# Layer norm ahead of linear attention and routed experts: 1/std by logarithm, exponential and a shorter Newton step, and the row normalisation split between VectorE and GpSimd

## What is computed

```python
xn = _layernorm(x)                       # (x - mean) / sqrt(var + 1e-5)
# attention: 16 heads of 8, feature map elu(a) + 1
q, k = elu(xn @ Wq.T) + 1, elu(xn @ Wk.T) + 1;  v = xn @ Wv.T
out = einsum(q, einsum(k, v)) / (q . sum(k) + 1e-6) @ Wo.T
# experts: 8 of them, one for each token
aff = xn @ centroids.T;  e = argmax(aff);  alpha = sigmoid(aff[e])
h = relu(_layernorm(xn, ln_g[e], ln_b[e]) @ w1[e].T + b1[e])
y = alpha * (xn + h @ w2[e].T + b2[e]) + (1 - alpha) * xn
```

## Time and profile before

| | us |
|---|---|
| median of 3 runs | 171.39 |
| lowest, highest | 169.41, 172.38 |
| time of the profiled execution | 170.78 |
| its span in the profile | 169.1 |
| busy: TensorE, VectorE, ScalarE, GpSimd | 139.1, 113.6, 104.9, 101.0 |

### The profile page before, as it was taken

How to read it: one execution, slowest core, us unless ns; L and a number is a source line. 1 busy time by engine, 2 the same in 40 slices (tenths; PEclk the granted TensorE clock), 3 DMA queues, 4 the chain that set the end, 5 groups by cost and what they waited for, 6 DMA issues and landing times.

```text
span 169.1 us, 4618 instructions
## 1 busy us (share of the span) xinstructions
PE 139.1 (82%) x1106; PEld 128.8 (76%) x1106; DVE 113.6 (67%) x411; ACT 104.9 (62%) x332; POOL 101.0 (60%) x108
## 2 busy tenths in 40 slices
PE   0066698999976987888799798999999999999950
PEld 0055597899944865766799688999999999999940
DVE  3899776999964865869756565666676665555540
ACT  8487996999252763556365647666676765566520
POOL 7600000899675655466235461888788868777884
PEclk9999999999999999999999999999999999999998
DMA  4999100680038765153234784698888878844433
GB/s 136 322 301 386 43 0 0 216 297 4 4 94 254 223 193 144 40 136 65 82 96 150 200 252 154 158 176 171 180 167 161 168 166 183 150 70 40 44 33 31
DMA packets 19113, 24.05 MB, mean 142 GB/s; under 512 B 2576, under 2 KB 13328, under 8 KB 18960
## 3 DMA queue, kind: packets, MB, share of 16 engines
q1 hardware_dynamic: 13456, 19.50, 36.2%
q0 software_dynamic: 5632, 4.26, 19.9%
HBM read 17.40 MB, written 6.36 MB: 140 GB/s over the span
## 4 chain that ended last, share of the span: by engine, by line
PE 53%; DVE 19%; issue 7%; ACT 7%; POOL 6%; another core or an unknown queue 2%; DMA 2%; DVEq 1%; ACTq 0%
PE bank L623 18%; PE bank L611 18%; POOL out L354 6%; PE bank L579 5%; PE bank L569 2%; ACT xn L401 2%; PE bank L596 2%; PE bank L515 2%; DVE feat_q L886 2%; PE bank L506 2%; PE bank L587 2%; DVE lane_neg L810 2%; PE bank L603 2%; DMA x<-in_x 2%
## 5 line engine op out<-in xcount | busy, mean ns | idle before, releaser
L470 ACT ACTIVATE hT<-bank,b 128x128 f32<-128x128 f32 x156 | 44.5, 368 | 29.6 <-PE bank L611 25.7
L354 POOL DMA_INDIRECT out<-rows,token_at x32 | 50.0, 1563 | 15.1 <-DVE rows L925 9.0
L346 POOL DMA_INDIRECT rows<-z_rows,token_at x32 | 30.6, 958 | 25.0 <-PE bank L611 11.5
L623 PE MATMUL bank<-w,hT 128*128 x312 | 42.8, 280 | 3.2 <-ACT hT L470 1.8
L623 PEld LDWEIGHTS bank<-w,hT 128*128 128x128 f32 x312 | 37.8, 191 | 5.2 <-issue 4.9
L611 PE MATMUL bank<-zT,feat_k 128*128 128x128 f32 x312 | 41.2, 275 | 0.0
L611 PEld LDWEIGHTS bank<-zT,feat_k 128*128 128x128 f32 x312 | 37.9, 192 | 0.0
L362 POOL TENSOR_TENSOR feat_k<-feat_k,k_exp 128x256 f32<-128x256 f32 x16 | 14.4, 920 | 24.8 <-ACT k_exp L449 24.3
L912 DVE TENSOR_SCALAR zT<-xn,ln_g,ln_b 128x128 f32 x39 | 13.7, 352 | 8.7 <-issue 7.6
L925 DVE SCALAR_TENSOR_TENSOR rows<-y_own,weight,rows 128x128 f32 x39 | 13.7, 351 | 7.7 <-DVE y_own L919 4.4
L579 PE MATMUL bank<-kv_all,feat_q 128*128 128x144 f32 x64 | 11.4, 300 | 6.9 <-DVE feat_q L886 5.5
(11 more groups left out here) (111 smaller groups left out, 228.9 us busy)
## 6 DMA issues: line engine op xcount, KB each, us to landing
feat_k<-in_w1T SPq DMA_DIRECT2D x39, 256.0 KB
z_rows<-xn SPq DMA_DIRECT2D x4, 528.0 KB, 5.8
w<-in_w2T SPq DMA_DIRECT2D x1, 2048.0 KB, 10.9
out<-x SPq DMA_DIRECT2D x8, 256.0 KB
x<-in_x SPq DMA_DIRECT2D x2, 768.0 KB, 7.0
x<-in_x SPq DMA_DIRECT2D x2, 256.0 KB, 2.9
b<-in_b SPq DMA_DIRECT2D x1, 512.0 KB, 6.5
rows<-z_rows,token_at POOLq DMA_INDIRECT x32
```

The lines of the kernel that those rows point to most:

```text
L346: g.indirect_dma_start(out=rows[:, t, :], out_offset=None, in_=z_dram, in_offset=bass.IndirectOffsetOnAxis(ap=token_at[:, t:t + 1], axis=0 ...
L354: g.indirect_dma_start(out=out_rows, out_offset=bass.IndirectOffsetOnAxis(ap=token_at[:, t:t + 1], axis=0), in_=rows[:, t, 0:D], in_offset ...
L470: last = a.activation(hT[:, par, c * P:(c + 1) * P], bank[hidden_bank(s)][:, c * P:(c + 1) * P], ACT.Relu, bias=b1[:, c, bass.ds(e, 1)])
L623: last = t_.matmul(bank[y_bank(s)][:, 0:D], hT[:, par, c * P:(c + 1) * P], w2[:, bass.ds(e * (FC * D) + c * D, D)], start=(c == 0), stop=( ...
```

## The change

- ScalarE computes `rough = exp(-0.5 ln(var + eps))` by two activations (Ln, Exp) in place of the square root; VectorE computes `var_half = -(var + eps)/2` and `rstd = rough (1.5 + rough² var_half)` in three dependent instructions in place of six with a reciprocal. `shift` and the two variance instructions are gone.
- ScalarE normalises no tile. GpSimd takes the last tile of each group (`XN_POOL` = 1), VectorE the other three, in every chunk. `transpose_x` and the store of the rows wait on GpSimd in place of ScalarE.
- The first `warm` takes Exp, the second is gone. `rough_rstd(1)` stands behind `copy_v(0)` and `copy_v(1)`, where `sqrt_of(1)` stood before them.
- The second norm has its own Ln and Exp on ScalarE (`rough_rstd_2`, behind the copies of `gr == 6`) and its own Newton step on VectorE, in `second_norm`, which stands now between the first and the second part of `choose`.
- GpSimd writes one more constant (`eps_ln`).

```diff
-    XN_ACT = (3, 2, 1)
+    XN_POOL = 1
...
+        ms_a, ms_b = sb("ms_a", [P, 3, TC]), sb("ms_b", [P, TC])
...
+        rstd = sb("rstd", [P, NT])
...
+            g.memset(eps_ln[:, :], EPS_LN).then_inc(eps_ready, 1)
...
+
+            def normalise(gr):
+
+                pool.wait_ge(rstd_ready, chunk_of(gr * TG) + 1)
+                for t in range((gr + 1) * TG - XN_POOL, (gr + 1) * TG):
+                    last = g.tensor_scalar(xn[:, t, 0:D], x[:, t, :], mean[:, t:t + 1], rstd[:, t:t + 1], ALU.subtract, ALU.mult)
+                last.then_inc(xn_by_pool, 1)
+
+            for gr in range(NG):
+                normalise(gr)
...
-            def sqrt_of(c):
+            def rough_rstd(c):
+
                 part = slice(CHUNK[c], CHUNK[c + 1])
                 act.wait_ge(var_ready, c + 1)
-                a.activation(std[:, :, part], var_e[:, :, part], ACT.Sqrt).then_inc(std_ready, 1)
+                a.activation(log_var[:, part], var[:, part], ACT.Ln, bias=eps_ln[:, 0:1]).then_inc(log_ready, 1)
+                act.wait_ge(log_ready, c + 1)
+                a.activation(rough[:, part], log_var[:, part], ACT.Exp, scale=-0.5).then_inc(rough_ready, 1)
...
+            def rough_rstd_2():
+
+                act.wait_ge(var_2_ready, 1)
+                a.activation(log_2[:, :], var_2[:, :], ACT.Ln).then_inc(log_2_ready, 1)
+                act.wait_ge(log_2_ready, 1)
+                a.activation(rough_2[:, :], log_2[:, :], ACT.Exp, scale=-0.5).then_inc(rough_2_ready, 1)
...
-            def normalise(gr):
-
-                act.wait_ge(rstd_ready, chunk_of(gr * TG) + 1)
-                for t in range(gr * TG, gr * TG + XN_ACT[chunk_of(gr * TG)]):
-                    last = a.activation(xn[:, t, 0:D], x[:, t, :], ACT.Identity, bias=shift[:, t:t + 1], scale=rstd[:, 0, t:t + 1])
-                last.then_inc(xn_by_act, 1)
...
             act.wait_ge(rows_ready, 1)
-            a.activation(warm[:, :], lane_row[:, 0:1], ACT.Sqrt)
+            a.activation(warm[:, :], lane_row[:, 0:1], ACT.Exp)
             expand_lanes()
-            sqrt_of(0)
-            normalise(0)
-            normalise(1)
+            act.wait_ge(eps_ready, 1)
+            rough_rstd(0)
             copy_xnT(0)
             copy_xnT(1)
-            sqrt_of(1)
             copy_v(0)
             copy_v(1)
-            normalise(2)
-            normalise(3)
+            rough_rstd(1)
             for gr in range(2, NG + LAG):
                 if gr < NG:
                     copy_xnT(gr)
                 if gr == 3:
-                    sqrt_of(2)
-                    a.activation(warm[:, :], mean[:, 0:1], ACT.Exp, scale=0.0)
-                if gr + 2 < NG:
-                    normalise(gr + 2)
+                    rough_rstd(2)
                 for j in range(TG // TB):
                     copy_v((gr - LAG) * TG // TB + j)
+                if gr == 6:
+                    rough_rstd_2()
...
-                pe.wait_ge(xn_by_act, gr + 1)
+                pe.wait_ge(xn_by_pool, gr + 1)
...
-                step(v_.scalar_tensor_tensor(ms_b[:, 0, 0:n], ms_a[:, 1, 0:n], 0.25, ms_a[:, 1, 0:n], ALU.mult, ALU.mult), filling)
-                step(v_.scalar_tensor_tensor(var, ms_a[:, 2, 0:n], 1.0 / D, ms_b[:, 0, 0:n], ALU.mult, ALU.add), filling)
-
-                v_.tensor_scalar(var_e[:, 0, part], var, 1.0, EPS_LN, ALU.mult, ALU.add)
-                v_.tensor_scalar(var_e[:, 1, part], var, 1.0 + EPS_LN, EPS_LN * EPS_LN, ALU.mult, ALU.add).then_inc(var_ready, 1)
+                step(v_.scalar_tensor_tensor(ms_b[:, 0:n], ms_a[:, 1, 0:n], 0.25, ms_a[:, 1, 0:n], ALU.mult, ALU.mult), filling)
+                v_.scalar_tensor_tensor(var[:, part], ms_a[:, 2, 0:n], 1.0 / D, ms_b[:, 0:n], ALU.mult, ALU.add).then_inc(var_ready, 1)
...
-                dve.wait_ge(std_ready, c + 1)
+                next(filling, None)
+                next(filling, None)
                 dve.wait_ge(var_ready, c + 1)
-                step(v_.reciprocal(rinv[:, :, 0:n], std[:, :, part]), filling)
-                step(v_.tensor_tensor(nw_a[:, :, 0:n], rinv[:, :, 0:n], rinv[:, :, 0:n], ALU.mult), filling)
-                step(v_.tensor_tensor(nw_b[:, :, 0:n], nw_a[:, :, 0:n], var_e[:, :, part], ALU.mult), filling)
-                step(v_.tensor_scalar(nw_a[:, :, 0:n], nw_b[:, :, 0:n], -0.5, 1.5, ALU.mult, ALU.add), filling)
-                step(v_.tensor_tensor(rstd[:, :, part], rinv[:, :, 0:n], nw_a[:, :, 0:n], ALU.mult), filling)
-                v_.scalar_tensor_tensor(shift[:, part], mean[:, part], -1.0, rstd[:, 0, part], ALU.mult, ALU.mult).then_inc(rstd_ready, 1)
+                v_.tensor_scalar(var_half[:, part], var[:, part], -0.5, -0.5 * EPS_LN, ALU.mult, ALU.add)
+                next(filling, None)
+                dve.wait_ge(rough_ready, c + 1)
+                step(v_.tensor_tensor(nw_a[:, 0:n], rough[:, part], rough[:, part], ALU.mult), filling)
+                step(v_.tensor_tensor(nw_b[:, 0:n], nw_a[:, 0:n], var_half[:, part], ALU.mult), filling)
+                v_.scalar_tensor_tensor(rstd[:, part], nw_b[:, 0:n], 1.5, rough[:, part], ALU.add, ALU.mult).then_inc(rstd_ready, 1)
+                next(filling, None)
+                dve.wait_ge(rstd_ready, c + 1)
...
-                    if t % TG >= XN_ACT[c]:
-                        ins = v_.tensor_scalar(xn[:, t, 0:D], x[:, t, :], mean[:, t:t + 1], rstd[:, 0, t:t + 1], ALU.subtract, ALU.mult)
-                        if t % TG == TG - 1:
+                    if t % TG < TG - XN_POOL:
+                        ins = v_.tensor_scalar(xn[:, t, 0:D], x[:, t, :], mean[:, t:t + 1], rstd[:, t:t + 1], ALU.subtract, ALU.mult)
+                        if t % TG == TG - XN_POOL - 1:
...
+            v_.tensor_scalar(var_2[:, :], var[:, :], 1.0 + EPS_LN, EPS_LN * EPS_LN, ALU.mult, ALU.add).then_inc(var_2_ready, 1)
...
-                v_.tensor_tensor(spread[:, :], var_e[:, 0, :], rstd[:, 0, :], ALU.mult).then_inc(chain, 1)
-                dve.wait_ge(chain, chained[0] + 1)
-                v_.tensor_tensor(xn[:, :, AT_C], spread[:, :], rstd[:, 1, :], ALU.mult).then_inc(meta_ready, 1)
+                dve.wait_ge(var_2_ready, 1)
+                v_.tensor_scalar(var_2_half[:, :], var_2[:, :], -0.5, None, ALU.mult)
+                v_.scalar_tensor_tensor(spread[:, :], var[:, :], EPS_LN, rstd[:, :], ALU.add, ALU.mult)
+                dve.wait_ge(rough_2_ready, 1)
+                step(v_.tensor_tensor(sq_2[:, :], rough_2[:, :], rough_2[:, :], ALU.mult), nothing)
+                step(v_.tensor_tensor(nw_2[:, :], sq_2[:, :], var_2_half[:, :], ALU.mult), nothing)
+                step(v_.scalar_tensor_tensor(rstd_2[:, :], nw_2[:, :], 1.5, rough_2[:, :], ALU.add, ALU.mult), nothing)
+                v_.tensor_tensor(xn[:, :, AT_C], spread[:, :], rstd_2[:, :], ALU.mult).then_inc(meta_ready, 1)
...
-            for c in range(len(CHOOSE) - 2):
+            choose(0)
+            second_norm()
+            for c in range(1, len(CHOOSE) - 2):
                 choose(c)
             dve.wait_ge(const_ready, 8)
             v_.tensor_copy(token_half[:, :], token_no[:, :]).then_inc(starts_full, 1)
-            second_norm()
```

More of the change, by code:

```diff
@@ L108, in linear_attention_and_routed_experts @@
         stats = sb("stats", [P, NT, 6])
[L109 to L116, removed]
+        ms_a, ms_b = sb("ms_a", [P, 3, TC]), sb("ms_b", [P, TC])
+        mean, var, var_half = (sb(n, [P, NT]) for n in ("mean", "var", "var_half"))
+        log_var, rough = sb("log_var", [P, NT]), sb("rough", [P, NT])
+        nw_a, nw_b = sb("nw_a", [P, TC]), sb("nw_b", [P, TC])
+        rstd = sb("rstd", [P, NT])
+        var_2, var_2_half, log_2, rough_2, sq_2, nw_2, rstd_2 = (
+            sb(n, [P, NT]) for n in ("var_2", "var_2_half", "log_2", "rough_2", "sq_2", "nw_2", "rstd_2"))
         spread = sb("spread", [P, NT])
+        eps_ln = sb("eps_ln", [P, 1])
         warm = sb("warm", [P, 1])
@@ L170, in linear_attention_and_routed_experts @@
             sem(n) for n in ("aug_ready", "rows_ready", "lane_full", "starts_full"))
-        stat_done, chain, var_ready, std_ready = sem("stat_done"), sem("chain"), sem("var_ready"), sem("std_ready")
-        xn_by_dve, xn_by_act, rstd_ready = sem("xn_by_dve"), sem("xn_by_act"), sem("rstd_ready")
+        stat_done, chain, var_ready, log_ready, rough_ready = (sem(n) for n in ("stat_done", "chain", "var_ready", "log_ready", "rough_ready"))
+        xn_by_dve, xn_by_pool, rstd_ready, eps_ready = sem("xn_by_dve"), sem("xn_by_pool"), sem("rstd_ready"), sem("eps_ready")
+        var_2_ready, log_2_ready, rough_2_ready = sem("var_2_ready"), sem("log_2_ready"), sem("rough_2_ready")
         xt_done, xnT_ready = sem("xt_done"), sem("xnT_ready")
@@ L272, in _ @@
             sp.wait_ge(meta_ready, 2)
-            sp.wait_ge(xn_by_act, NG)
+            sp.wait_ge(xn_by_pool, NG)
             sp.wait_ge(xn_by_dve, NG)
@@ L691, in moments @@
                 st = stats[:, part, :]
-                var = ms_b[:, 1, 0:n]
```

## The result

The changed kernel took 182.24 us (median of 4 runs, 180.52 to 182.62) against 170.70 (also 4 runs) for the kernel before on the same chip: ratio 1.065, 95% interval 1.0592 to 1.0709. It is slower by some 11 us. The range ended at 173.6. What happened is rival 1: each Ln and each Exp was given a load of its own.

What follows compares the result with a forecast made beforehand. ScalarE was on the chain in the norm; VectorE was taken as the new bound. The terms 0.15 + 0.35 - 0.33 = +0.17 on the profiled 170.78 gave 170.95, say 171.0 us, range 168.8 to 173.6.

Steps and rivals of the forecast that it cites:

- rival 1: ScalarE's tables swapped back and forth, one load for each Ln and Exp: 8.1 us more, so 179; chance 0.16.
- Chunk 0: Swapped tables at the first chunk's norm: Ln's load partly hidden (0.8 left), Exp's load 1.28 in full.
- Chunk 1: Swapped tables at the second chunk's norm: both loads, Ln's and Exp's, wholly on the chain, 2.56 us.
- Chunk 2: Swapped tables at the third chunk's norm: Ln's load wholly hidden, Exp's load costing 1.28 us.
- The last pair: Swapped tables at the second norm's Ln and Exp, in front of copy_xnT(7): some 2.2 of 2.56 us.
- The forecast's own case: One table load for Ln and Exp, a GpSimd tile costing VectorE 0.1 to 0.45: 171.0 us; chance 0.51.
- the mark: Start of group 5's transposes, first of the last chunk: forecast at 22.05 against 21.91 before, 0.15 later.
- k: What one GpSimd normalisation tile costs VectorE: taken as 0.3 us, between 0 and 0.51; each 0.1 moves group 5's transposes by 0.6.
- The tie in chunk 1: VectorE wants `rough` just when ScalarE, behind copy_v(1), gets to it, so that wait costs 0.
- `rough_rstd(2)` was to find ScalarE waiting: Third chunk's norm: ScalarE reaches this step before the variance is there, so VectorE's chain sets the time.
- After the mark: Past group 5's transposes: second norm's Ln and Exp add 0.35, two VectorE instructions gone save 0.33.
- The claim that ScalarE's 5 us would be no gain by themselves: In the norm, 3.8 us of tiles and a 1.28 table load leave ScalarE, but VectorE becomes the bound.

Runs made afterwards that it cites:

- e1: Changed kernel with one hand-placed load of a table for both Ln and Exp, in place of nine loads: 162.07 against 161.60 us, ratio 1.0014.
- after_again: The changed kernel itself, unedited, timed again on the chip of the second series: 182.26 us, ratio 1.0673 to the kernel before.
- e5: e1 with two table loads put back, ahead of the second norm's Ln and Exp alone: 173.48 against 171.13 us, ratio 1.0151.
- e6: e1 with rough_rstd(1) moved ahead of the first copies of v and rough_rstd(2) ahead of copy_xnT(3): 169.58 us, ratio 0.9912.
- e3: Kernel before with only the tile split changed: VectorE three of each group, GpSimd one, ScalarE none: 162.98 us, ratio 1.0082.
- e4: e1 with ScalarE normalising 3, 2 and 1 tiles per group, GpSimd none, rough_rstd(1) in sqrt_of(1)'s place: 160.42 us, ratio 0.9899.
- e8: e6 with ScalarE taking 3 and 2 tiles per group in chunks 0 and 1, none in chunk 2 (GpSimd one, VectorE three): 166.87 us, ratio 0.9841.

## Why the prediction was wrong

**The step that failed** is the number of table loads: the sum was added up for one load, with no term for eight more, and rival 1, which had them, was weighed at 0.16. The runs show the eight loads as the whole loss, some 11 us: with them the ratio is 1.065 and 1.067, without them (e1) 1.0014. "Nothing in this trace" spoke against the rival, and nothing in it spoke for the forecast: that Ln and Exp would share one load, and that the program would hold no other, was my assumption, and no row showed it. The runs show that the two are different things. e1 served both functions with one load (1.28 us at 0.81), so a table for both exists; the changed kernel, left as it was written, has nine loads, eight of them in front of one Ln or one Exp each. The trace of before held no evidence either way on a rival of 8 us, against a forecast of no change; an even chance would have been honest.

**Rival 1's own price** was 8.1 us; the eight loads cost some 11 by the ratios (after_again against e1). Its terms, against the delays between the traces of e1 and the changed kernel (taken on different chips):

- Chunk 0 was put at 2.1, since a load seemed not to wait with its activation. The load began at 6.36, behind the variance, and the first tile is at 10.11 against 7.54 in e1, the full 2.57. The load at 0.81 that I had read it from the earlier trace rows stands at the head of ScalarE's program, and says nothing of later ones.
- Chunk 1 was put at 2.56. The delay at its Newton step is 18.87 - 14.31 = 4.6, so it cost 2.0; in e1 the values had waited 0.6 for their weights, and here they were there.
- Chunk 2 was put at 1.28, with the load for Ln hidden. The delay at its Newton step is 28.26 - 21.00 = 7.3, so it cost 2.7. The variance was done at 23.85, but ScalarE came to the load only at 25.11, behind copy_xnT(3), and nothing of it was hidden.
- The last pair was put at 2.2; e5 measured 2.3. In the changed kernel the delay at the scan is 40.77 - 30.82 = 9.95 in one profiled execution and 43.01 - 30.82 = 12.19 in the other, so the pair cost 2.7 and 4.9 there. What no term had is TensorE behind that pause, the 2.2 between the two.

**The forecast's own case**, which e1 is, gave +0.1% and measured +0.14%. Its steps, by the trace of e1: first tile of VectorE at 7.54 (7.6 was forecast); bn_stats of chunk 1 at 9.22 (9.7); tiles of chunk 1 at 15.15 (14.9); the mark at 22.68 (22.05). At the scan e1 is 0.6 behind the kernel before (30.82 against 30.23), though its time is the same. So part of this agreement is luck: a k that was too large (by 0.2, and so six tiles' worth, 1.2 us, too late) stood against two waits that the sum left out (2.5 us too early). The errors one by one:

- k, the cost of a GpSimd tile to VectorE, was 0.3. Six tiles beside two of GpSimd's took 1.85 against 1.62 for six alone, nine beside three 2.58 to 2.65 against 2.39: k is 0.06 to 0.12. A GpSimd tile itself lasts 2.52/3 = 0.84, twice the select that I took as its nearest row. Had such a tile held VectorE up for its whole length, it would have cost 0.84; the rows show no such thing.
- The tie in chunk 1 was none. VectorE waited 1.01 for `rough_rstd(1)` behind the copies of v. TensorE's values began at 11.23, when their weights `cent_wv` had landed (7.16 us of transfer in the chain), and not after the transposes. The sum had no term for that transfer.
- `rough_rstd(2)` was to find ScalarE waiting. It was the other way round: VectorE waited 1.50, since copy_xnT(3), ahead of it, came late behind transposes of 1.06 where I had none of TensorE's time in the sum.

e6 takes the first wait away and most of the second, and wins 1%, which shows them as real costs of the change's order. "After the mark" was right to 0.2: from the mark to the scan e1 takes 8.14, the kernel before 8.32, where +0.02 was forecast. The second norm's VectorE instructions moved off the chain.

**The claim that ScalarE's 5 us would be no gain by themselves** stands for the tiles, 3.8 of the 5: e3 moved them and lost 0.8%. For the 1.28 of the table load no run tests it alone.

## What to carry to other kernels

When a change brings a function that the trace has not shown, ask first which table each activation will find loaded, and count the loads in the program; here a pair of loads lasted 2 x 1.28 = 2.6 us at each use, and cost 2.0 to 4.9 where its result was waited for. With the table loaded by hand the change as it was written was worth nothing (e1); its arithmetic with the tiles left on ScalarE was worth 1% (e4), the whole with ScalarE's order mended 0.9% (e6), and with the tiles' places fitted as well 1.6% (e8). ScalarE ran its instructions in the order of the code, and moving `rough_rstd` ahead of copies was worth 1% (e6 against e1): put the short step that another engine waits for ahead of copies that only feed the same engine's later work.

## What was not expected of the hardware

- A table load behind a wait began only when the wait was over (6.36, with the variance done at 6.28), though its row names no tile that it reads.
- A GpSimd tile of 128x128 with two pointer columns takes 0.84 us, nearly as long as an addition of twice the size (0.92), and yet costs VectorE's tiles beside it only 0.1 (six in 1.85 us beside two of them, 1.62 alone).
- After a pause of 2.69 us TensorE ran the same 16 matmuls in 1.95 us in one execution and 3.62 in another, with the granted clock at 1.00 and 0.63 to 0.69; the price of this pause differed from run to run. From 20 to 25 the matmuls of both executions are equally slow (four transposes in 1.1), while the granted clock reads 1.00 in the first and 0.50 in the second; there the record of the clock is less to be trusted than the matmuls' own times. So that the clock made the difference behind the pause of 2.69 is likely, by the records of two executions, and no run tests it.
